# A graph layer's schedule: edge rounds loaded ahead of the weights, bases in two steps, the first three blocks as single groups

## The reference

```python
h = relu(layernorm(x))                                     # x: 6250 x 128
agg = segment_sum(edge_attr, dst, num_segments=6250)       # edge_attr: 106250 x 128, dst sorted
hid = relu(concatenate([agg, h], axis=1) @ W1 + b1)        # W1: 256 x 512
out = x + hid @ W2 + b2                                    # W2: 512 x 128
```

## Time and profile before

| | us |
|---|---|
| median of 3 runs | 219.62 (219.38 to 221.08) |
| the profiled execution | 219.51 |
| its span, first to last instruction | 217.4 |
| TensorE busy | 191.9 (88%) |
| VectorE busy | 132.7 (61%) |
| ScalarE busy | 83.7 (38%) |
| POOL busy | 43.5 (20%) |
| DMA moved | 62.54 MB, mean 288 GB/s |

### The profile page before, as it was taken

How to read it: one execution, slowest core, us unless ns; L and a number is a source line. 1 busy time by engine, 2 the same in 40 slices (tenths; PEclk the granted TensorE clock), 3 DMA queues, 4 the chain that set the end, 5 groups by cost and what they waited for, 6 DMA issues and landing times.

```text
span 217.4 us, 6713 instructions
## 1 busy us (share of the span) xinstructions
PE 191.9 (88%) x2525; PEld 163.3 (75%) x2525; DVE 132.7 (61%) x579; ACT 83.7 (38%) x181; POOL 43.5 (20%) x120
## 2 busy tenths in 40 slices
PE   1326979989889999999999999999999999999970
PEld 0214868769669889889798898898988988978860
DVE  2532777797887767747747567477575684751110
ACT  3131045253253361383343623823535238234300
POOL 4464112220220222112202211122022112200000
PEclk9999999999999999999999999999999999999997
DMA  6999999999999998999989999999999970100101
GB/s 216 302 372 372 376 374 376 376 377 377 384 376 311 368 351 280 370 348 310 379 292 384 374 316 377 322 309 362 311 383 375 292 265 7 51 0 3 48 3 39
DMA packets 44590, 62.54 MB, mean 288 GB/s; under 512 B 1763, under 2 KB 44262, under 8 KB 44556
## 3 DMA queue, kind: packets, MB, share of 16 engines
q1 hardware_dynamic: 43150, 60.78, 80.6%
q10 hardware_dynamic: 1406, 1.30, 1.8%
HBM read 58.88 MB, written 3.20 MB: 286 GB/s over the span
## 4 chain that ended last, share of the span: by engine, by line
PE 69%; DVE 11%; DMA 7%; issue 3%; ACT 2%; SPq 1%; DVEq 1%; POOL 1%; ACTq 0%; POOLq 0%
PE bank L754 19%; PE bank L698 17%; PE bank L733 13%; PE bank L742 13%; DMA edges<-in_edge_attr 7%; DVE onehot L430 3%; PE bank L709 3%; DVE aggT L512 2%; PE bank L719 2%; ACT agg_hi L359 1%; DVE agg_lo L470 1%; ACT hidden L369 1%; DVE halves L443 1%; DVEq L496 1%; PE bank L691 1%
## 5 line engine op out<-in xcount | busy, mean ns | idle before, releaser
L698 PE MATMUL bank<-edges,onehot 128*32 128x128 f32 x1656 | 54.2, 285 | 6.6 <-DMA edges<-in_edge_attr 6.1
L698 PEld LDWEIGHTS bank<-edges,onehot 128*32 128x32 f32 x1656 | 46.0, 114 | 14.5 <-DMA edges<-in_edge_attr 7.8
L754 PE MATMUL bank<-w,hidden 128*128 128x128 f32 (+1 forms) x400 | 48.2, 278 | 0.7 <-ACT hidden L369 0.7
L754 PEld LDWEIGHTS bank<-w,hidden 128*128 128x128 f32 (+1 forms) x400 | 45.5, 189 | 3.5 <-issue 3.4
L369 ACT ACTIVATE hidden<-bank,b_col 128x512 f32<-128x512 f32 (+2 forms) x52 | 33.8, 663 | 36.6 <-PE bank L742 36.5
L338 ACT ACTIVATE xn<-xs,shift,rstd 128x128 f32<-128x128 f32 (+1 forms) x50 | 21.8, 484 | 62.8 <-POOL shift L302 62.8
L512 DVE TENSOR_TENSOR aggT<-bank,aggT 128x32 f32 x277 | 35.5, 189 | 15.9 <-issue 9.1
L295 POOL TENSOR_SCALAR var<-meanvar 128x2 f32<-128x2 f32 (+1 forms) x25 | 7.3, 293 | 138.6 <-DVE meanvar L448 138.6
L430 DVE TENSOR_TENSOR onehot<-relT,iota 128x384 f32<-128x384 f32 x69 | 34.3, 551 | 0.4 <-ACT iota L373 0.4
L464 DVE TENSOR_TENSOR hT_lo<-bank,hT_hi 128x256 fp32r<-128x256 f32 (+1 forms) x25 | 10.4, 415 | 19.0 <-ACT hT_hi L345 19.0
L733 PE MATMUL bank<-hT_hi,w_hi 128*128 128x512 f32 (+2 forms) x52 | 21.2, 408 | 0.0
(11 more groups left out here) (91 smaller groups left out, 166.9 us busy)
## 6 DMA issues: line engine op xcount, KB each, us to landing
edges<-in_edge_attr SPq DMA_DIRECT2D x69, 768.0 KB, 8.5
out_rows<-outrow SPq DMA_DIRECT2D x11, 256.0 KB
xs<-in_x SPq DMA_DIRECT2D x21, 128.0 KB, 8.6
w<-in_L_gnn_W ACTq DMA_DIRECT2D x1, 512.0 KB, 7.4
xs<-in_x ACTq DMA_DIRECT2D x1, 384.0 KB, 3.6
hidden<-in_dst SPq DMA_DIRECT2D x2, 192.0 KB, 5.6
w<-in_L_gnn_W ACTq DMA_DIRECT2D x1, 256.0 KB, 10.5
out_rows<-outrow SPq DMA_DIRECT2D x2, 128.0 KB
```

Source lines behind the costliest of these rows:

```text
L698: ins = nc.tensor.matmul(sums_ps[t * W:(t + 1) * W, cols], onehot[:, hots, e, :], edges[:, slot, e * F:(e + 1) * F], start=(g == 0), stop= ...
L754: ins = nc.tensor.matmul(out_ps[0:w, (2 * i + j) * F:(2 * i + j + 1) * F], hidden[:, t, at:at + w], w2[:, t, :], start=(t == 0), stop=(t = ...
```

## The change

- SP issues two rounds of edges ahead of W1, a third ahead of x of blocks 1 and 2, two more ahead of W2, then the other three. ScalarE's queue issues x of block 0 alone, the other receivers, b1 and b2. The last rows of x are loaded by SP at k = 21.
- The bases of the first 128 chunks are turned and written to `base_tab` right after the first receivers' turn; those of the others follow.
- Blocks 0, 1 and 2 are groups of their own (256 columns wide, output halves of `outrow` in turn, each with its own store and semaphore), then pairs (3,4), (5,6) and so on. For k = 1, 2, 3 TensorE runs these small layers between the rounds of block k.
- In every iteration VectorE now begins with `rest_of_h(k - 1)`, then `add_sums(k - 1)`, and takes `stats(k + 1)`; TensorE runs `turn_x(k)` ahead of `turn_sums(k)`; ScalarE runs `h_out(k - 1)` and `normalise(k + 1)`.
- The test's parts move to k = 6, 7, 8, 9 and 11. POOL clears most of `aggT` before the first scale and shift.

```diff
-            for r in range(1, RING):
+            load(1)
+            sp.dma_start(w1[:, :, :], W1.rearrange("(t p) h -> p t h", p=P)).then_inc(w1_landed, 16)
+            load(2)
+            sp.dma_start(xs[:, 1:3, :], x_v[:, 1:3, :]).then_inc(x_next_landed, 16)
+            load(3)
+            load(4)
+            sp.dma_start(w2[:, :, :], W2.rearrange("(t p) f -> p t f", p=P)).then_inc(w2_landed, 16)
+            for r in range(5, RING):
                 load(r)
...
+                if k + 3 == NB - 1:
+                    sp.dma_start(xs[0:NLAST // 2, NB - 1, :], x_last_v).then_inc(x_last_landed, 16)
+                early = k <= EARLY + 1
+                if early and group2(k - 1) is not None:
+                    store(group2(k - 1), group2(k - 1))
...
-                if k >= 3 and k % 2 == 1:
-                    store((k - 3) // 2, (k - 3) // 2)
+                if not early and group2(k - 1) is not None:
+                    store(group2(k - 1), group2(k - 1))
...
+            clear(0, 1)
+            pool.wait_ge(rel_ready, 1)
+            clear(1, 6)
+            pool.wait_ge(rel_ready, 4)
+            spread(0)
+            clear(6, CLEARS)
+            for b in range(1, NB):
                 spread(b)
...
+            normalise(0)
+            act.wait_ge(rel_turned, 3)
+            act.wait_ge(rel_copied, 5)
+            nc.scalar.activation(b1_col[:, :], misc_ps[:, 96:96 + HT], ACT.Copy).then_inc(b1_ready, 1)
+            h_out(0)
+            copy_sums(0)
+            act.wait_ge(b1_ready, 1)
+            for k in range(1, NB):
+                early = k <= EARLY
+                if k >= 2:
+                    h_out(k - 1)
+                if not early:
+                    copy_sums(k)
+                round_agg(k - 1, chunks_by(k - 1), place(k - 1), group_of(k - 1))
+                if group1(k) is not None:
+                    relu(group1(k), group1(k))
+                if k == 1:
+                    normalise(1)
+                if early:
+                    copy_sums(k)
+                if k + 1 < NB:
+                    normalise(k + 1)
+            h_out(NB - 1)
...
+            dve.wait_ge(bases_turned, 1)
+            nc.vector.tensor_scalar(base_tab[:, 0:P], row_ps[0:1, 0:P], 0.0, float(N - 1), ALU.max,
+                                    ALU.min).then_inc(bases_ready, 1)
+            stats(0)
...
+            rest_of_h(0)
+            dve.wait_ge(rel_copied, 5)
+            build(ROUNDS[1][0])
+            stats(1)
+            dve.wait_ge(bases_ready, 3)
+            bases = load_bases(0)
+            for k in range(1, NB):
+                if k >= 2:
+                    rest_of_h(k - 1)
+                if k == 1:
+                    dve.wait_ge(agg_cleared, CLEARS)
+                add_sums(k - 1, bases)
+                if k == 1:
+                    for r in ROUNDS[1][1:]:
+                        build(r)
+                rest_of_agg(k - 1, k - 1, place(k - 1))
...
-                if k + 2 < NB:
-                    stats(k + 2)
-                if k + 1 < NB:
-                    add_b2(k + 1)
-                if k == 2:
+                    stats(k + 1)
+                add_b2(k - 1)
+                if k == 6:
                     dve.wait_ge(limit_ready, 1)
                     overrun(colA, relA, limit[:, 0:1])
-                if k == 3:
+                if k == 7:
                     overrun(colB, relB, limit[:, 1:2])
-                if k == 4:
+                if k == 8:
                     overrun(colC, relC, limit[0:CC, 2:3])
                     overrun(colD, relD, None)
-                if k == 5:
+                if k == 9:
                     apart = w1[0:1, 0, 0:FULL - 1]
...
+                if k == FLAG:
...
+            rest_of_h(NB - 1)
             add_sums(NB - 1, bases)
             rest_of_agg(NB - 1, NB - 1, place(NB - 1))
...
             turn_ab(0, relA).then_inc(rel_turned, 1)
+            turn_column_a(0).then_inc(bases_turned, 1)
+            sum_rounds(0, 0, 2)
+            pe.wait_ge(rel_ready, 2)
...
+            pe.wait_ge(bases_ready, 1)
+            turn_columns_bc(0).then_inc(bases_turned, 1)
+            sum_rounds(0, 2, 3)
             turn_x(0)
-            for k in range(NB):
-                sum_rounds(k)
...
+            turn_sums(0)
+            for k in range(1, NB):
+                one, two = group1(k), group2(k)
...
+                if k <= EARLY:
+                    sum_rounds(k, 0, 1)
+                    if two is not None:
+                        layer2(two, two)
+                        sum_rounds(k, 1, 2)
+                    layer1_h(one, one)
+                    layer1_agg(one, one, blocks_of(one)[-1] + 1)
+                    sum_rounds(k, 1 if two is None else 2, 4)
+                    turn_x(k)
+                    turn_sums(k)
+                else:
+                    sum_rounds(k)
+                    if two is not None:
+                        layer2(two, two)
+                    if one is not None:
+                        layer1_h(one, one)
+                    turn_x(k)
+                    turn_sums(k)
+                    if one is not None:
+                        layer1_agg(one, one, blocks_of(one)[-1] + 1)
+                if k == FLAG:
```

More of the change, by code:

```diff
@@ L82, in place @@
     def place(b):
-        first = BLOCK if b and b % 2 == 0 else 0
+        first = BLOCK if b >= ONES and (b - ONES) % 2 else 0
         return slice(first, first + 2 * width(b))
@@ L204, in graph_layer @@
         over_read = sem("over_read")
+        stored_one = [sem(f"stored_one{i}") for i in range(2)]
         stored = sem("stored")
@@ L281, in _ @@
                 sp.dma_start(edges[0:KREST, 0, 0:GR * F], rest_v).then_inc(wide_landed, 16)
-                store(NS, 0)
-                with sp.Fori(1, NS - 1) as s:
+                for s in range(ONES):
+                    store(NS + s, s)
+                with sp.Fori(ONES, NS - 1) as s:
                     store(NS + s, s)
                 store(2 * NS - 1, NS - 1)
-                sp.wait_ge(stored, 16 * (2 * NS + 2))
+                sp.wait_ge(stored, 16 * (2 * NS - ONES + 2))
         @block.gpsimd
@@ L315, in _, with clear @@
             n = NWIDE * WIDE // CLEARS
-            for i in range(CLEARS):
-                nc.gpsimd.memset(aggT[:, i * n:(i + 1) * n], 0.0).then_inc(agg_cleared, 1)
-                if i < 2:
-                    spread(i)
-            for b in range(2, NB):
+            def clear(first, last):
+                for i in range(first, last):
+                    nc.gpsimd.memset(aggT[:, i * n:(i + 1) * n], 0.0).then_inc(agg_cleared, 1)
+            clear(0, 1)
[5 more added lines that the diff above has]
+            for b in range(1, NB):
                 spread(b)
@@ L404, in again_group @@
                     relu(n, s)
-                again_group(NS, 0)
-                with act.Fori(1, NS - 1) as s:
+                for s in range(ONES):
+                    again_group(NS + s, s)
+                with act.Fori(ONES, NS - 1) as s:
                     again_group(NS + s, s)
@@ L541, in _ @@
             relative(0, dstA, colA, relA)
-            stats(0)
             dve.wait_ge(rel_turned, 1)
@@ L655, in again_group @@
                     finish(n, s)
-                again_group(NS, 0)
-                with dve.Fori(1, NS - 1) as s:
+                for s in range(ONES):
+                    again_group(NS + s, s)
+                with dve.Fori(ONES, NS - 1) as s:
                     again_group(NS + s, s)
@@ L828, in again_group @@
                     layer2(n, s)
-                again_group(NS, 0)
-                with pe.Fori(1, NS - 1) as s:
+                for s in range(ONES):
+                    again_group(NS + s, s)
+                with pe.Fori(ONES, NS - 1) as s:
                     again_group(NS + s, s)
```

164 lines of the change are left out of this document (72 added, 92 removed).

## The result

| | before | changed |
|---|---|---|
| median | 219.5 us (219.16 to 221.08) | 243.3 us (241.2 to 245.11) |
| the profiled execution | 219.51 | 244.11 |
| its span | 217.4 | 242.2 |
| TensorE busy | 191.9 (88%) | 199.7 (82%) |

What follows compares the result with a forecast made beforehand. TensorE bounds the kernel from 61.5 us on, edges and VectorE's adds before. Beginning -3.1, ring +18.4, tests +2.3 and end +1.0 take the span from 217.4 to 236.0; plus 2.1 makes 238 us, range 230 to 243.

Steps and rivals of the forecast that it cites:

- the ring: Steady part: way from hT_lo round the engines takes 16.7 us per two blocks against TensorE's 14.66; +18.4 us over nine periods.
- The two halves of the ring: hT_lo to next hT_lo: 8.1 us from odd block through VectorE and POOL, 8.6 from even block through TensorE.
- rival 3: Clock falls in TensorE's new gaps, layer1_h taking 6.0 us instead of 3.0: 265 us, or 245 to 265; chance 0.04.
- the 2.0 us per period: TensorE's forecast idle time in front of layer1_h in each two-block period of the steady part.
- The tests: Overrun tests on VectorE ahead of hT_lo: +0.4 at k = 6, +1.5 at 8, nothing at 7 and 9, 0.4 at 11; together +2.3.
- The beginning: Up to layer 1's aggregate half of block 5: at 58.4 instead of 61.52, -3.1 us; bounds -5.6 and +1.
- Round 3: Block 0's fourth edge round on TensorE: start at 18.6 instead of 19.48, 0.9 us earlier for fewer bytes ahead.
- The slow early layers: Block 0's layer 1 at half rate: hT_lo of block 1 about 2.4 us later, sum 240.4; none of it taken.
- The end: At block 24 layer1_h waits for x turned just before: +1.0 on 24.0 us after the nine periods.
- The sum: Profiled span: 58.4 + 150.3 + 2.3 + 24.0 + 1.0 = 236.0 us; 2.1 more gives 238 us.
- Rivals 1 and 2: TensorE stays the bound, 214 us, chance 0.06; or a ring of 15 to 16 us, 221 to 230 us, chance 0.08.
- Rival 4: At the start the rounds land no sooner: +1 instead of -3.1, 242 us, inside the range; no chance of its own.

Runs made afterwards that it cites:

- Experiment 2: The kernel before, with only VectorE's order changed: hT_lo of block k ahead of the adds of block k-1; 235.87 us, ratio 1.073.
- experiment 1: The changed kernel with the adds of block k-1 put ahead of its hT_lo again on VectorE; 231.89 us, ratio 1.058.
- 4: experiment 1 with hT_hi, hT_lo and the statistics made one block earlier from block 7 on, as before the change; 222.87 us, ratio 1.014.
- experiment 5: The changed kernel with hT_hi copied ahead of the next block's normalisation and hT_lo taken at the end of its own iteration; 220.78 us, ratio 1.007.
- experiment 9: experiment 6 with hT_lo ahead of the output add, and the overrun tests between the adds and agg_lo (last parts at 14 and 15); 214.34 us, ratio 0.977.
- experiment 3: The changed kernel with seven more matmuls, results overwritten, in front of layer1_h's wait for hT_lo; 239.45 us, ratio 1.091.
- 11: experiment 3 with the parts of the overrun test at odd blocks 7, 9, 11 and 13; 234.95 us, ratio 1.072.
- Experiment 7: The kernel before with only the changed kernel's order of the first transfers; 217.75 us, ratio 0.993.
- experiment 6: experiment 5 with the overrun test's parts at even iterations 6, 8, 10 and 12, and their read-out ahead of layer 2; 220.3 us, ratio 1.007.

## Why the prediction was right, and where it was off

*The sign and the mechanism* were right: 243.3 against 238, slower, by the ring named ahead. But the median is 0.3 us over the top of the range (the runs lie from 241.2 to 245.11).

*The two halves of the ring*, 8.1 and 8.6, measured 7.97 and 8.70: 16.67 for 16.7, closer than the halves, whose two errors have opposite signs. Experiment 2 shows the exchange of adds and hT_lo alone, experiment 1 its undoing, 4 and 5 that of hT_hi behind xn. Together with 9, where neither is in the way and TensorE is again unbroken, the cause of the steady loss is shown.

*The step that failed is the clock's.* The prediction gave rival 3 a chance of 0.04, and argued from one hole, that before 61.52, behind which the layer took no longer. The hole in the kernel before ended ahead of the transposes, and not at 61.52 as I wrote:

```profile
60.67 0.52 PE L709 MATMUL bank<-ident,sums 128*128 128x128 f32 x3 [1.57 <-DVE aggT L512]
```

It was 1.57 us long, the new ones 1.1 to 3.8; one shorter case was no evidence for longer ones, and the 2.0 us per period that I had worked out myself should have told so. The fall came in part: one `layer1_h` before block 5's L802 and three behind it ran slow, not all nine. And it was cheaper than the 3.0 us that I gave it in each period (6.0 instead of 3.0): 1.3 to 1.55 us, since the clock was full again before the group ended; 5.8 us in all. The Trainium skill (TensorE: Matmul & The Clock Gate, "Why this matters for your kernels") warns of idle gaps between bursts of matmuls that bring the low clock back. The trace agrees with it by the four rows at 0.50 and 0.51, but the gaps it warns of are longer than three of these four holes and than the 2.0 us that I forecast, so its words alone would not have told that these holes do it. Experiments 3 and 11 show the cost by filling the holes: 3.9 us less with one slow stretch left, and no slow stretch once the tests are moved too.

*The tests.* At k = 6, 0.5 us for 0.4; at k = 8, 2.0 for 1.5 (the half ring took 9.97); at k = 7 nothing, as said; at k = 11 some 0.1 where I put 0.4 (the half ring took 10.19, of it 1.4 the clock). Here they are on VectorE in the changed kernel, the third test's start, the late output add and the late hT_lo:

```profile
87.15 0.53 DVE L582 TENSOR_REDUCE colC<-relC 20x1 f32<-20x384 f32 x1
...
91.00 0.69 DVE L542 TENSOR_TENSOR outrow<-bank,xs 128x512 f32<-128x512 f32 x1 [0.86 <-issue]
...
91.60 0.41 DVE L511 TENSOR_TENSOR hT_lo<-bank,hT_hi 128x256 fp32r<-128x256 f32 x1
```

It made the longest hole, 3.81 us before 92.16, and that one a slow stretch: the period of 20.22.

*The beginning.* Two errors met and cancelled, by luck. Round 3 was mis-sized: I counted only the bytes that leave from in front of it, 0.9 us, and it came 2.8 earlier:

```profile
16.63 1.51 PE L758 MATMUL bank<-edges,onehot 128*32 128x128 f32 x24 [0.58 <-DMA edges<-in_edge_attr]
```

Experiment 7 has 16.69 from the transfers' order alone. Against that, the blocks from 1 to 3 were 8.56 us apart, not 8.1 and 7.6. Hence hT_lo of block 4 at 54.24, forecast 54.3. Then `layer1_h` fell into the first slow stretch, and L802 came at 59.69, not 58.4. Round 3's rate, 1.51 us for its 24 rows, was again half, though the granted clock is given as 1.00 there. The slow early layers that I left out came in part: `layer1_h` of block 0 took 2.85 us in the chain, against 1.62 for block 1, but its aggregate half 1.43, and not the 2.8 that the 2.4 us hung on. hT_lo of block 1 came at 29.15, before the 30.5 forecast.

*The end*: 242.2 - 217.27 = 24.9 us, forecast 25.0.

*The sum.* 236.0 forecast for the span. L802 of block 5 is 1.3 late (clock 1.55, the rest earlier). The nine periods are 157.6 against 150.3 + 2.3 = 152.6: 5.0 more, of it clock 4.3, tests 0.2 and 0.5 spread over the halves (estimates by difference). The end -0.1. That is 242.2.

*Rivals 1 and 2* did not come in this kernel, but the runs show what they would have needed: 1 gave 214 for TensorE as the bound, and experiment 9, where it is, took 214.34. That the two agree so well is luck: 9 is another kernel, with tests and h in other places and 0.85 us more around its last blocks. *Rival 4* fell with round 3.

## What to carry to other kernels

Before reordering streams that work in order, walk once round from an operation to its next instance over all engines, with rows for each leg, and compare it with the bound engine's work: an operation that waits must not stand ahead of one that is ready (adds behind hT_lo, hT_hi behind the next xn, hT_lo behind an output add that waits for a store). Compare leg by leg, and not only the sum: in experiment 1 one half was TensorE's and the other the ring's, and the period was longer than either whole. A gain at the beginning survives only if every stream keeps its slack behind it. And where a reordering opens holes in TensorE, price what the holes do to the rate of the work behind them.

## What the runs showed of the hardware that I had not expected

- A hole's length alone did not tell whether the granted clock fell. In the changed kernel holes of 2.85, 3.81, 2.56 and 2.57 us were followed by 0.5, others of 2.57 (at 162.21), 2.31 and 2.15 us were not; in experiment 2 one of 1.57 us was (0.73 over the stretch from 47.50 to 50.90, after three matmuls at the full rate), in the kernel before one of 1.57 us was not, and neither were one of 2.64 us in experiment 1 and one of 3.08 us in experiment 5. Each fall in the changed kernel cost 1.3 to 1.55 us of one layer. What decides between them stays open.
- TensorE doing useless work made the kernel faster: seven matmuls per pair, 1.83 us each time, took off 3.9 us (experiment 3).
- A store of output rows took 9.96 us from issue to landing (experiment 6), about as long as the loads of edges ahead of it on SP's queue, whose median was 9.0. The Trainium skill (DMA: Bandwidth & Descriptors, "Queues, rings and completion order") says that each DMA engine takes the descriptors of a ring in their order; the two numbers agree with it, though no run here put the stores on another queue.
- The new order of the first transfers, which leaves 0.3 MB less in front of round 3, brought it 2.8 us forward (experiment 7), three times what those bytes at 360 GB/s come to. It also put W1 behind round 1 and the other receivers into ScalarE's queue, and round 1 already came some 3 us earlier; which of these did it was not tried.
